# A language-model tower on one core: in the back pipeline, part of the gate's sum moves to GpSimd, an eviction and a reduction move to ScalarE, and TensorE's work is reordered

## The reference, cut to what matters

```python
# end of layer 0: gates of the four experts from the graph's scores (top 2 of 4), then
h = h + sum_e gate[e] * y[e]            # y: expert outputs, (tokens, 4, 64)
x2 = layernorm(h);  h = h + x2
# attention of 16 heads, 4 channels each; k and v normed in each head
q, k, v = x2 @ Wq + bq, ln(x2 @ Wk + bk), ln(x2 @ Wv + bv)
kvm = (k^T v) / 256, heads apart        # one 64x64 matrix for each batch row
h = h + gelu((q @ kvm + x2) @ Wp + bp)
x3 = layernorm(h);  h = h + x3          # the third norm
# MLP with routing: 127 of 256 tokens of each batch row are kept
r = x3 @ wr + br
y = gelu_tanh(x3 @ W1 + b1) @ W2 + b2
out = h + keep(r) * r * y
```

## Time and profile before

| | us |
|---|---|
| median of 3 runs | 5198.41 (5193.08 to 5199.17) |
| the profiled execution's own time | 5155.78 |
| its span, first to last instruction | 5154.0 |
| busy: PE, DVE, ACT, POOL | 3124.6, 2843.2, 2310.2, 2223.9 |
| mean granted clock of PE | 0.719 |

### The profile page before, as it was taken

One profiled execution on the slowest core, in us unless ns is written; L12 is line 12 of the kernel. 1 busy time (PEld: TensorE's weight loads), 2 busy tenths in 40 slices (PEclk: granted clock), 3 DMA queues, 4 the chain that ended last, 5 costly groups with the idle time before them and its releaser, 6 DMA issues. The chain is left out here.

```text
span 5154.0 us, 63155 instructions
## 1 busy us (share of the span) xinstructions
PE 3124.6 (61%) x21213; PEld 2411.5 (47%) x21213; DVE 2843.2 (55%) x5880; ACT 2310.2 (45%) x3968; POOL 2223.9 (43%) x2218
## 2 busy tenths in 40 slices
PE   3656554656656566566566566565665665627885
PEld 2445443445445445445454454454454444515664
DVE  8967872435445445445354354454454453578775
ACT  3656654444444434434444444344344344215554
POOL 7876603443443443434434434434334344354420
PEclk7666766777777777777777777777777777755666
DMA  1111101110111111111111111111111111021101
GB/s 58 24 25 21 21 21 25 28 30 23 29 28 23 34 24 26 31 23 27 31 23 27 30 23 30 27 25 32 24 26 31 23 27 31 15 74 36 36 2 33
DMA packets 157528, 145.16 MB, mean 28 GB/s; under 512 B 71240, under 2 KB 133080, under 8 KB 156776
## 3 DMA queue, kind: packets, MB, share of 16 engines
q1 hardware_dynamic: 88656, 109.52, 6.4%
q0 software_dynamic: 68768, 34.45, 6.2%
HBM read 93.00 MB, written 50.82 MB: 28 GB/s over the span
## 5 line engine op out<-in xcount | busy, mean ns | idle before, releaser
L937 PE MATMUL es_pgot<-hash_space,es_pick 128*128 128x256 bf16 x13056 | 1835.9, 288 | 1425.4 <-issue 1403.0
L857 POOL DMA_INDIRECT es_got<-node_table,late x1632 | 1548.0, 949 | 2130.6 <-DVEq L1077 1653.3
L937 PEld LDWEIGHTS es_pgot<-hash_space,es_pick 128*128 128x128 bf16 x13056 | 1304.4, 101 | 1898.9 <-issue 1739.7
L1019 DVE TENSOR_TENSOR es_prod<-es_pgot,es_own 128x512 f32<-128x512 f32 x272 | 187.8, 690 | 1804.8 <-PE es_pgot L937 1621.4
L871 ACT ACTIVATE es_pick<-es_away,consts 128x512 bf16<-128x512 f32 x1088 | 680.0, 711 | 7.1 <-DMA es_away<-sorted_keys 6.7
L293 POOL DMA_INDIRECT fr_ring<-in_emb,fr_rows x384 | 459.4, 1196 | 178.8 <-issue 113.7
L875 ACT ACTIVATE es_pick<-es_pick,consts 128x4096 bf16<-128x4096 bf16 x136 | 503.6, 3703 | 0.9
L894 ACT ACTIVATE ex_hid<-ex_phid,weights 128x256 f32<-128x256 f32 x128 | 53.6, 470 | 691.1 <-PE ex_phid L944 690.7
L1039 DVE TENSOR_TENSOR es_hot<-es_iota,late 128x1024 bf16<-128x1024 f32 x272 | 331.8, 1220 | 33.4 <-DVE es_st L1079 25.7
L1040 DVE TENSOR_TENSOR es_hot<-es_iota,late 128x1024 bf16<-128x1024 f32 x272 | 330.5, 1215 | 0.0
L1021 DVE TENSOR_REDUCE es_got<-es_prod 128x32 f32<-128x512 f32 x272 | 275.9, 1014 | 39.6
(11 more groups left out here) (346 smaller groups left out, 4427.4 us busy)
## 6 DMA issues: line engine op xcount, KB each, us to landing
es_away<-sorted_keys SPq DMA_DIRECT2D x68, 512.0 KB
es_got<-node_table,late POOLq DMA_INDIRECT x1632
edge_states<-es_st SPq DMA_DIRECT2D x68, 384.0 KB
expert_outputs<-ex_y SPq DMA_DIRECT2D x64, 256.0 KB
bk_y<-expert_outputs SPq DMA_DIRECT2D x8, 2048.0 KB
fr_ring<-in_emb,fr_rows POOLq DMA_INDIRECT x384
out_dram<-h SPq DMA_DIRECT2D x4, 1024.0 KB, 5.1
weights<-in_weights SPq DMA_DIRECT2D x1, 2079.0 KB, 13.6
```

Of the source, the lines that this page charges most:

```text
L857: pool.indirect_dma_start(out=got[:, r, k, :], out_offset=None, in_=table_dram, in_offset=bass.IndirectOffsetOnAxis(ap=src[:, n, k:k + 1]. ...
L937: mm = pe.matmul(p_got[:, q, c * 256:c * 256 + 256], pick[:, r, q // 2, k, at * P:at * P + P], parts[:, part, k], start=(k == 0 and part = ...
```

## The change

- LAG goes from 5 to 4, so there are 36 steps. The output's bias no longer comes with DVE's eviction: PE puts it into PSUM with one bf16 product (3 x 256) ahead of the second MLP product, from a new tile `bias_y` that DVE prepares by a further call of `exact_rows` (64 wide). ACT evicts the product, after q, with a plain copy.
- The second MLP product (16 instructions, L1731) is issued in two halves with the attention output (L1740) between them; q (L1736) comes behind the second half.
- The third norm's squares and sums: four ACT squares of 128 x 64 with an accumulated output take the place of one of 128 x 256 (L1452) and DVE's reduction (L1658). They stand behind ACT's new eviction.
- `gate_join` and `gate_rows` go to GpSimd: in steps with q = 1 behind two gathers and ahead of the addition of x2, and for group 0 ahead of the last 12 of the 40 gathers issued before the loop. DVE's `norm_centre` waits for them.
- The selection's first transposes are issued by PE in the last step, ahead of the last slot's second MLP product, and no longer wait for all outputs.

```diff
-LAG = 5
+LAG = 4
...
-        p_w, p_kept = b_xt[0:B, 0:T], b_xt[:, T:T + 2 * B].rearrange("p (two b) -> p two b", two=2)
+        p_w, p_kept = b_q[0:B, 0:T], b_q[:, T:T + 2 * B].rearrange("p (two b) -> p two b", two=2)
...
+            def gate_rows(g):
+                pool.wait_ge(s_used, g + 1)
+                nc.gpsimd.tensor_tensor(total[:, :, 0], total[:, :, 0], total[:, :, 1], ALU.add).then_inc(s_joined, 1)
+                pool.wait_ge(s_joined, g + 1)
+                nc.gpsimd.tensor_tensor(h[:, tiles(g)], h[:, tiles(g)], total[:, :, 0], ALU.add).then_inc(s_rows, 1)
+
             for n in range(-10, 0):
+                if n == -3:
+                    gate_rows(0)
                 gathers(n, range(ST))
...
                 gathers(n, range(2))
+                if q == 1 and g + 1 < GN:
+                    gate_rows(g + 1)
                 if is_slot(new):
...
                 if is_slot(mlp):
-                    act.wait_ge(s_sum3, mlp + 1)
+                    act.wait_ge(s_sum3, (mlp + 1) * ST)
...
                     a.activation(qt[:, new % 2], p_q, ACT.Identity, bias=W("q_b")).then_inc(s_qt, 1)
+                if is_slot(last):
+                    act.wait_ge(s_y_p, last + 1)
+                    a.activation(xc[:, slot(last)], p_y, ACT.Copy).then_inc(s_y, 1)
                 if is_slot(joined):
                     act.wait_ge(s_xc3, joined + 1)
-                    if joined >= 1:
-                        act.wait_ge(s_sum3, joined)
-                    a.activation(sq3[:], xc[:, slot(joined)], ACT.Square).then_inc(s_sq3, 1)
+                    for t in range(ST):
+                        col = joined * ST + t
+                        a.activation(sq3[:, t], xc[:, col], ACT.Square, accum_out=rstd3[:, col:col + 1]).then_inc(s_sum3, 1)
...
             def gate_total(g):
                 y = y_in[g % 2]
-                do(v.tensor_tensor(total[:], y[:, :, 0:2], y[:, :, 2:4], ALU.add))
-                dve.sem_inc(s_used, 1)
...
+                if g >= 1:
+                    dve.wait_ge(s_rows, g)
+                v.tensor_tensor(total[:], y[:, :, 0:2], y[:, :, 2:4], ALU.add).then_inc(s_used, 1)
+
+            def norm_centre(g):
                 t = tiles(g)
+                dve.wait_ge(s_rows, g + 1)
...
+            exact_rows(do, v, bias_y[:], W("m_b2"), part[:, 0:D], rest[:, 0:D], exact[:, 0:D], C)
...
-                if q == 1:
-                    (gate_total, gate_join, gate_rows)[part](g + 1)
+                if q == 1 and part == 0:
+                    gate_total(g + 1)
...
-                if is_slot(done):
-                    dve.wait_ge(s_y_p, done + 1)
-                    v.tensor_tensor(xc[:, slot(done)], p_y, repeat(W("m_b2"), ST), ALU.add).then_inc(s_y, 1)
...
-                if is_slot(joined):
-                    dve.wait_ge(s_sq3, joined + 1)
-                    v.tensor_reduce(rstd3[:, slot(joined)], sq3[:], AX.X, ALU.add).then_inc(s_sum3, 1)
...
-            dve.wait_ge(s_y, SLOTS)
             dve.sem_inc(s_w, 1)
...
             dve.wait_ge(s_hx3, SLOTS)
+            dve.wait_ge(s_y, SLOTS)
...
+            def outputs(these):
+                for t in these:
+                    for m in range(2):
+                        mm = pe.matmul(p_y[:, t, :], hid[:, m, t * P:t * P + P], W("m_w2")[:, m * D:m * D + D], start=False, stop=(t == ST - 1 and m == 1))
+                return mm
...
-                    if new - LAG >= 0:
-                        pe.wait_ge(s_y, new - LAG + 1)
+                    if new - LAG >= 1:
+                        pe.wait_ge(s_y, new - LAG)
...
+                if last == SLOTS - 1:
+                    pe.wait_ge(s_w, 1)
+                    for half in range(2):
+                        mm = pe.transpose(p_w[:, half * P:half * P + P], rw[:].rearrange("p (b two) -> p two b", two=2)[:, half], C("ident"))
+                    mm.then_inc(s_w_p, 1)
                 if is_slot(last):
...
-                    for t in range(ST):
-                        for m in range(2):
-                            mm = pe.matmul(p_y[:, t, :], hid[:, m, t * P:t * P + P], W("m_w2")[:, m * D:m * D + D], start=(m == 0), stop=(m == 1))
-                    mm.then_inc(s_y_p, 1)
+                    pe.matmul(p_y.rearrange("p t d -> p (t d)"), ones[0:3], repeat(bias_y[0:3], ST), start=True, stop=False)
+                    outputs((0, 1))
+                if is_slot(normed):
+                    pe.wait_ge(s_kvm, normed + 1)
+                    pe.wait_ge(s_qt, normed + 1)
+                    pe.matmul(p_o, kvm[:], qt[:, normed % 2], start=True, stop=True).then_inc(s_o_p, 1)
+                if is_slot(last):
+                    outputs((2, 3)).then_inc(s_y_p, 1)
                 if is_slot(new):
                     if joined >= 0:
                         pe.wait_ge(s_gj, joined + 1)
                     pe.matmul(p_q, W("q_w"), xt[:, new % 2], start=True, stop=True).then_inc(s_q_p, 1)
-                if is_slot(normed):
-                    pe.wait_ge(s_kvm, normed + 1)
-                    pe.wait_ge(s_qt, normed + 1)
-                    pe.matmul(p_o, kvm[:], qt[:, normed % 2], start=True, stop=True).then_inc(s_o_p, 1)
```

More of the change, by code:

```diff
@@ L1288, in back @@
         kvm, gj, sq3 = sb("kvm", [P, P]), sb("gj", [P, 2, 2, SB, D]), sb("sq3", [P, ST, D])
-        bias, ones = sb("bias", [P, SB * 2 * D + D], BF16), sb("ones", [P, P], BF16)
+        bias, bias_y, ones = sb("bias", [P, SB * 2 * D + D], BF16), sb("biasy", [P, D], BF16), sb("ones", [P, P], BF16)
         part, rest, exact = (sb(n, [P, SB * 2 * D + D]) for n in ("part", "rest", "exact"))
@@ L1301, in back @@
         p_x3, p_rw = b_x3[:, 0:T], b_x3[:, T:T + TILES].rearrange("p (s two b) -> p s two b", two=2, b=SB)
-        p_w, p_kept = b_xt[0:B, 0:T], b_xt[:, T:T + 2 * B].rearrange("p (two b) -> p two b", two=2)
+        p_w, p_kept = b_q[0:B, 0:T], b_q[:, T:T + 2 * B].rearrange("p (two b) -> p two b", two=2)
         (s_var, s_norm, s_kvm, s_rt, s_x2, s_xc3, s_sum3, s_x3, s_y, s_bias, s_dve) = (
             sem(n) for n in ("var", "norm", "kvm", "rt", "x2", "xc3", "sum3", "x3", "y", "bias", "dve"))
-        (s_xt, s_sq, s_qt, s_std, s_gj, s_sq3, s_std3, s_x3t, s_hid) = (
-            sem(n) for n in ("xt", "sq", "qt", "std", "gj", "sq3", "std3", "x3t", "hid"))
+        (s_xt, s_sq, s_qt, s_std, s_gj, s_std3, s_x3t, s_hid) = (
+            sem(n) for n in ("xt", "sq", "qt", "std", "gj", "std3", "x3t", "hid"))
         (s_xt_p, s_kv_p, s_q_p, s_kvm_p, s_o_p, s_prj_p, s_x3_p, s_hid_p, s_y_p, s_rw_p) = (
             sem(n) for n in ("xtp", "kvp", "qp", "kvmp", "op", "prjp", "x3p", "hidp", "yp", "rwp"))
-        s_hx2, s_kv, s_hx3, s_sd = (sem(n) for n in ("hx2", "kv", "hx3", "sd"))
+        s_hx2, s_kv, s_hx3, s_sd, s_joined, s_rows = (sem(n) for n in ("hx2", "kv", "hx3", "sd", "joined", "rows"))
         s_var_g, s_std_g, s_less, s_exp, s_read, s_xc2, s_sq2, s_sum2, s_std2, s_used = (
@@ L1359, in _ @@
                 new, normed, mlp = n, n - 1, n - 3
+                g, q = divmod(n, GS)
                 gathers(n, range(2))
+                if q == 1 and g + 1 < GN:
+                    gate_rows(g + 1)
                 if is_slot(new):
@@ L1530, in gate_total @@
                 y = y_in[g % 2]
-                do(v.tensor_tensor(total[:], y[:, :, 0:2], y[:, :, 2:4], ALU.add))
-                dve.sem_inc(s_used, 1)
-            def gate_join(g):
-                do(v.tensor_tensor(total[:, :, 0], total[:, :, 0], total[:, :, 1], ALU.add))
-            def gate_rows(g):
-                t = tiles(g)
-                do(v.tensor_tensor(h[:, t], h[:, t], total[:, :, 0], ALU.add))
+                if g >= 1:
+                    dve.wait_ge(s_rows, g)
+                v.tensor_tensor(total[:], y[:, :, 0:2], y[:, :, 2:4], ALU.add).then_inc(s_used, 1)
             def norm_centre(g):
                 t = tiles(g)
+                dve.wait_ge(s_rows, g + 1)
                 do(v.tensor_reduce(mean2[:, t], h[:, t], AX.X, ALU.add))
@@ L1601, in _ @@
                     gate_total(0)
-                    gate_join(0)
-                    gate_rows(0)
                     norm_centre(0)
@@ L1606, in _ @@
             for n in range(STEPS):
-                new, normed, joined, mlp, done = n, n - 1, n - 2, n - 3, n - LAG
+                new, normed, joined, mlp = n, n - 1, n - 2, n - 3
                 g, q = n // GS, n % GS
-                if is_slot(done):
-                    dve.wait_ge(s_y_p, done + 1)
-                    v.tensor_tensor(xc[:, slot(done)], p_y, repeat(W("m_b2"), ST), ALU.add).then_inc(s_y, 1)
                 if is_slot(new):
@@ L1762, in _ @@
                     mm.then_inc(s_prj_p, 1)
-            pe.wait_ge(s_w, 1)
-            for half in range(2):
-                mm = pe.transpose(p_w[:, half * P:half * P + P], rw[:].rearrange("p (b two) -> p two b", two=2)[:, half], C("ident"))
-            mm.then_inc(s_w_p, 1)
             pe.wait_ge(s_kept, 1)
```

## The result

| | before | after |
|---|---|---|
| median (five runs each, side by side) | 5193.08 us (5185.65 to 5199.17) | 5224.47 us (5218.40 to 5229.44) |
| ratio | | 1.0065, 95% interval 1.0052 to 1.0078 |
| profiled execution, its span | 5154.0 | 5222.4 |
| of it: back pipeline, from DVE's first instruction (the memset of `bk_ones`) on | 601.5 | 635.6 |

The change makes the kernel 31 us slower; the forecast was 12 us faster. In the two profiled executions the stages ahead of the back pipeline, which the change does not touch, differ by 34.3 us (it begins at 4586.8, not 4552.5). I read this as a difference of the two executions and compare the back pipeline alone: 34.1 us longer, which fits the medians' 31.4.

What follows compares the result with a forecast made beforehand. It took no engine as full: a chain of waits, x3 - PE - rt - DVE, bounds, and after the change x3 - PE - q - ACT. Terms summed to 16.8 - 57 f, -12 us at f = 0.5: 5187 us, range 5150 to 5214.

Steps and rivals of the forecast that it cites:

- The clock share: Share f of time PE runs at its fast clock in loop and late steps; taken as 0.5, total 16.8 - 57 f.
- PE's clock near 0.7: Sign to look for in the profile after: PE's granted clock near 0.7 between 4670 and 5020 us.
- The price: What a fast clock is worth in the 23 loop steps: 42 us less for a fast share of one.
- Rival 2: PE's clock stays as in the loop or lower, f 0.2 to 0: +5 to +17, 5203 to 5215 us; chance 0.2.
- the start: Before the loop, the last gathers wait behind GpSimd's two additions: +5.3 us.
- The bias product: Bias product on PE ahead of the attention output: 0.39, a little overlapped, so 0.3 us a step.
- GpSimd's part: Gate additions on GpSimd, 2.4 us each, once in a group; GpSimd's work behind them costed at nothing.
- the port: DVE's L1626 waits for GpSimd's SBUF access once a group: 2.4 us, or 3.2 where ACT does not delay DVE.
- Rival 3: The port costs DVE the whole of both additions, 6.5 us a group: +22, 5209 us; chance 0.15.
- ACT takes the place of DVE: At low clock DVE waits for ACT every step; loop 14.6 us, savings of 2.1 + 0.7 shrink to about 1.2.
- The late steps: Five steps without gate work: 73.0 us all slow, 58.0 all fast, against 59.3 now, so +13.7 - 15 f.
- The end: Steps 32 and 33 lose 3 us to ACT's eviction wait; the selection starts earlier, -4.5 us.

Runs made afterwards that it cites:

- e4: The changed kernel with 12 unread bfloat16 filler products added on PE ahead of each wait for x3; ratio 1.0021 to the kernel before, back part 606.1 us.
- e5: The changed kernel itself, unchanged, run again as a control; ratio 1.0099 to the kernel before, back part 627.0 us.
- e1: The changed kernel with the gate's join and residual additions put back from GpSimd on DVE; ratio 1.0003 to the kernel before, back part 603.2 us.
- e14: The changed kernel with PE's bias product for the MLP output left out; ratio 1.0016 to the kernel before, back part 606.3 us.
- e3: The changed kernel with ACT's root for the gates issued ahead of its root for k and v; ratio 1.0084 to the kernel before.
- e17: The changed kernel with PE's old order (whole second MLP product, q, attention output); ratio 1.0048 to the kernel before, back part 622.5 us.
- e8: The kernel before with PE's new order alone (attention output between the second product's halves, q behind both); ratio 0.9946 to the kernel before, back part 573.2 us.
- e12: The kernel before with PE's new order and the four squares with sums on ACT; ratio 0.9937 to the kernel before, back part 572.7 us.
- e13: The changed kernel with the MLP output's eviction on DVE, not ACT, bias product kept; ratio 1.0071 to the kernel before, back part 621.4 us.
- e10: The kernel before with only the gate's join and residual additions moved to GpSimd; ratio 1.0043 to the kernel before, back part 615.8 us.
- e2: The changed kernel with q ahead of the second product's second half, ACT's squares before q's eviction, output eviction behind it; ratio 0.9997 to the kernel before.
- e18: The changed kernel with one square on ACT and the sums on DVE again; ratio 1.0049 to the kernel before, back part 622.9 us.

## Why the prediction was wrong

Forecast -12, range -48 to +16; measured +31 (median), +34.1 in the profile.

- **The clock share, f = 0.5: wrong, and by the prediction's own prices the largest error.** "PE's clock near 0.7" was 0.50 in the loop of the first profile and 0.56 in the second. With f = 0 in the loop and 0.22 in the late steps (0.61) the prediction's own sum is +13.5 and not -12: 25 of the 46 us between it and the profile's +34.1. The failed step is its argument, "PE is busier than in the present late steps, and in those half of the time was fast". PE is busier and gets less clock: busy 0.82 of the time at 0.61 before, 0.91 at 0.50 after. The price was of the right order where filler raised the clock (e4: 57 for a share of one, 42 forecast); e5 against after shows 12, and e1 steps in which the clock gave nothing, so the 25 us are the prediction's own arithmetic and not a measured share. Rival 2 had f = 0.2 to 0 and 5203 to 5215; it is nearest to the truth, and still 9 us short. The 20.6 that are left are 13.3 in the loop, 4.4 at the start, 2.8 late and 0.1 at the end.
- **The bias product: 0.3 forecast, 0.63 measured** (e14 and its rows). It is the 0.3 by which steps of 14.6 became 14.9; over 28 steps 9 us.
- **The wait of L1508 for the gate's root: left out.** Five steps of the loop are 1.5 longer for it, 7.5 us; moving the root (e3) took 0.8 of the 1.5 back.
- **GpSimd's part: right.** Additions 2.35 (2.4 forecast), the port 2.3 (2.4), the start +6.2 in e5 (+6.3 with step 1). The sum for slow steps gave DVE's saved 1.2 a group no worth, and e1 bears that out. Rival 3 (both additions in full) did not happen.
- **ACT takes the place of DVE: right.** Loop 14.6 forecast, 14.9 measured; L1627 waits for L1424 in all steps but those with q = 3. The late steps took 72.9; 73.0 was the forecast for a clock that is always slow, and at the 0.61 measured its sum gives 69.7. The prediction took it as a gain that shrinks from 2.8 to 1.2 a step. e17 shows that here the gain is gone altogether.
- **The end: right.** -1.5 forecast, -1.4 measured. The selection's first copy on VectorE in after, 1.2 us behind the last router product (5177.26 + 1.01):

```profile
5179.46 0.42 DVE L1664 COPY bk_w<-bk_pq 64x256 f32<-64x256 f32 x1 [0.80 <-PE bk_pq L1733]
```

- **The start:** +6.3 forecast, +6.2 in e5; the 4.5 more of the first profile stay open.

So the parts do not add up. Alone they come to +14.3 + 13.4 - 28.3 - 7.7 = -8 us by the back parts, and by the ratios to 0.43 + 0.61 - 0.54 - 0.08 = 0.42%, 15 us, give or take 11; together they come to +25 to +34. Five of the kernels stand in one line, each with one part more than the last, and show where it happens:

| | back | ratio | loop steps in which DVE's reciprocal waits for ACT |
|---|---|---|---|
| before | 601.5 | 1 | 0 of 23 |
| with PE's order (e8) | 573.2 | 0.9946 | 6 |
| and the squares (e12) | 572.7 | 0.9937 | 9 |
| and the eviction, the bias product, LAG 4 and the selection (e1) | 603.2 | 1.0003 | 18 |
| and GpSimd's additions, the whole change (e5) | 627.0 | 1.0099 | 18 |

PE's order shortens DVE's path and puts q, and so ACT, close behind it. The eviction with its bias product then lays 0.63 on PE and 0.3 on ACT, all on that chain, and costs 30 us (23 by the ratios) where alone it cost 13 (21): DVE's 0.35 a step that it spares is worth nothing there (e13 gives the eviction back to DVE and is not slower), as are the 1.2 a group that go to GpSimd (e1, e10). For the squares a turn from gain to loss is seen in the late steps only; for the whole kernel it is not shown. e2, which takes q and the squares off that chain, gets back the whole loss, 1.4 in a step at the same clock.

What stays open is what the clock follows. The Trainium skill (TensorE: Matmul & The Clock Gate, Part 1) has it rise when PE is busy and fall when it idles. Of the trace that holds only in part: filler in the pauses does raise it, but the stretch of 15 us with hardly a pause stayed at 0.50.

## What to carry to other kernels

When one edit moves the bound from engine A to engine B, work that other edits move from A to B turns from a gain into a loss: price each part against the loop that bounds after all of them, and try the reordering alone first (here 0.9946). A small product in front of a long one on the bounding engine costs its gaps too: here 0.63 us for a product recorded with 0.39. Take rows of the same kind of step when two kernels are compared. And never let a granted clock that isn't in the trace carry the sign of a forecast: give the sum for the lowest level as the main case.

## What was not expected of the hardware

- 12 unread bfloat16 products a step made a loop bound by fp32 products 19 us shorter, with a granted clock of 0.73 and not 0.56, and the late steps of the kernel before ran at 1.00 with them (53.7 us, not 59.7).
- A fuller PE did not get more clock: 0.91 busy at 0.50, against 0.82 at 0.61.
- ScalarE's four squares of 128 x 64 with a sum, with no bias operand, take 1.07 us, 0.24 from start to start.
- At the start of the changed kernel some eight tiny VectorE instructions take 4.7 to 5.4 us more in the three profiles beside the longer stages (after, e17, e18), and nothing more in the others; the kernel before shows none there.
